# A graph and expert network on one core: two LSTM streams, and the ODE layer beside a VectorE recurrence

## The chip, the cores and the metric

The kernel runs on one core of a Trainium2 chip. A core has TensorE (matrix products, results in PSUM), VectorE (DVE), ScalarE (ACT), GpSimd (POOL) and SyncE (SP, which here starts the DMAs). Each engine runs its own list of instructions in order; they meet only at semaphores. The metric is the device time of one execution in microseconds (us). TensorE's clock is granted in two levels, 1.2 and 2.4 GHz; the profile gives the mean as a share of the higher.

## What is computed

Eight residual blocks over x of 16 batches x 512 nodes x 128 features. Each takes the layer norm of x and adds its result to x. Two of them matter here, the diffusion LSTM and the Euler steps of an ODE, and of a third the eigenvectors of the graph's Laplacian:

```python
# 1: diffusion LSTM
h = relu(einsum('ts,bsh->bth', adj, x @ Wg0 + bg0))
h = relu(einsum('ts,bsh->bth', adj, h @ Wg1 + bg1))
for p in range(1, 5):
    nw = T // p
    wins = h[:, :nw * p, :].reshape(B * nw, p, H)
    last = lstm_last(Wih[p-1], Whh[p-1], bih[p-1], bhh[p-1], wins)   # p steps
    h = h.at[:, arange(nw) * p + (p - 1), :].set(last.reshape(B, nw, H))
# 3: ODE, after the first expert layer
h = einsum('bnd,ed->bne', x, fc_in_w) + fc_in_b
for _ in range(8):
    f = alph * 0.5 * (adj @ h - h) + h @ w_eff - h + x0
    h = h + f / 8
# 5: spectral
_, U = eigh(L_norm)
```

## The kernel before

The whole network is one program. Nothing is loaded in between but weights: x stays in SBUF as X, 64 tiles of 128 nodes x 128 features (GT = 4 tiles a batch). The stages follow one another: the Laplacian is made tridiagonal; `diffusion_lstm`; the first expert layer, beside which VectorE and ScalarE count eigenvalues; in `eigenvectors` a recurrence for the vectors and their joining; the product with the reflections; `ode`; two expert layers with the spectral layer between; attention; the last expert layer.

`diffusion_lstm` runs a hardware loop over 8 pairs of batches. TensorE makes adj x (L2262), times the first weights (L2267 and L2268), times the second (L2273), times adj (L2279), and then the recurrences of p = 1 to 4. The 512 nodes of a pair's two batches are columns. `steps` lists eleven turns: p = 1 for each batch, then p = 2, 3, 4 with one turn for each t, both batches side by side, 2 x (512 // p) columns. A turn has three or four gates. For each, TensorE adds the input part (Wih, L2287, which reads HL at a stride of p columns) and, for t > 0, the state part (Whh, L2302). ScalarE puts the gate through a sigmoid or tanh into `gt` (L2336); VectorE makes the cell CC (L2224 to L2233), ScalarE its tanh (L2341), VectorE the state or, in a chain's last turn, the columns of HL (L2241). The next turn's state part waits for that. There are two sets of four PSUM banks (PG, PAB), and the input part of turn t + 1 goes into the other set while the gates of turn t are read. At the end TensorE turns HL around (L2310) and VectorE adds it to X. All of the pair's buffers exist once, and the next pair starts when `x_done` comes. An fp32 matmul is two passes, and the profile counts passes.

In `eigenvectors`, VectorE runs a recurrence over 512 nodes, for four eigenvalues a partition, from both ends of the matrix: q = d - lambda - e2 / q'. The forward and backward halves are 4 numbers each. Before it, DN is filled with the diagonals and e2 for all nodes (L908 to L916). A hardware loop over 32 blocks of 16 nodes copies a block of DN to `dn` (L923), does for each node STT, TT and RECIPROCAL for either half (L933, L937, L942) in `qr`, and copies `qr` to QR (L945). Behind it are operations on four rows of 512 (from L958), the scaling of V by G (L1016 to L1032) and the joining of the parts (from L1058). TensorE has nothing here.

`ode` rewrites the eight Euler steps as polynomials in M = L1 (the mixing matrix) with coefficients Gm and Fr (from powers R). Preparation: layer norm statistics of X (L1353); TensorE transposes L1 (L2458) and makes the products L2T, L3T, L6T (L2464), copied from PSUM by ScalarE (L2389), and small rows (L2495 to L2503). Then come 17 turns, g = -1 for the constant part and 0 to 15 for the batches: TensorE multiplies YT by Gm (L2551), transposes the next batch (L2557), applies M to UU (L2563), makes the next batch's L3T rows (L2570), applies M to VV, and makes the L6T rows. VectorE copies UU (L2517) and VV (L2526), normalises batch g + 2 (`normalize`, L1399), adds KC to X (L2523) and adds the result (L2530). ScalarE copies YT (L2539).

## Time and profile before

| | us |
|---|---|
| runs | 7629.35, 7630.39, 7633.64 |
| median | 7630.39 |
| the profiled execution: its own time | 7630.28 |
| its span in the trace | 7628.1 |
| TensorE busy | 5332.3 (70%) |
| VectorE busy | 4702.8 (62%) |
| ScalarE busy | 2291.0 (30%) |

No engine is busy throughout. The shares of the whole span say little, since the stages have different limits; they have to be read stage by stage. A row of stretches gives for each engine what it was busy for in one, and the granted clock. A row of the timeline gives the start of a run of like instructions, its length, the engine, the line, the operation, its operands and its shape; in square brackets, how long the engine had stood and what released it. "PEq", "DVEq" and "ACTq" there are the engines' own sequencers, which held the instruction back for a semaphore.

### The profile page before, as it was taken

Reading aid. Unit: us, or ns where it says so; the run is one execution under the profiler, and the core shown is the slowest. Engines: PE = TensorE matmul, PEld = TensorE weight load, DVE = VectorE, ACT = ScalarE, POOL = GpSimd, SP = SyncE. Lnnn points to the kernel's source line nnn. Section 1 sums busy time; section 2 is a strip of 40 time slices with the busy share of each in tenths; the row PEclk is TensorE's granted clock in tenths of the full one; section 3 lists DMA queues with packets and bytes.
Section 4 is the critical chain, followed back from the end, with each engine's and each line's share of the span. In section 5 each row is a group of like instructions: output and inputs, shape, how many; then the busy total and the mean of one; then the engine's idle time right before and its main releaser. Section 6 shows DMA issues by size and latency. Waiting matters only on the chain. (4 is left out here: it accounts for less than half of the span.)

```text
span 7628.1 us, 113557 instructions
## 1 busy us (share of the span) xinstructions
PE 5332.3 (70%) x33091; PEld 3818.8 (50%) x33091; DVE 4702.8 (62%) x29590; ACT 2291.0 (30%) x7310; POOL 17.9 (0%) x36
## 2 busy tenths in 40 slices
PE   5777666555555688869899940048966679966899
PEld 5656555555444344446566630025644247744676
DVE  7878888787887422249999999952135333342433
ACT  1222222222222233329699850001012023310333
POOL 0000000000000000000000000000000000000000
PEclk9999999999999988869999975579978879987799
DMA  0000000000000000010000000000001000000000
GB/s 35 2 2 2 2 2 2 1 1 1 1 1 1 18 0 0 0 48 5 4 5 5 5 1 0 0 7 1 1 6 40 1 11 0 0 8 12 0 0 22
DMA packets 23193, 47.92 MB, mean 6 GB/s; under 512 B 5673, under 2 KB 16322, under 8 KB 20930
## 3 DMA queue, kind: packets, MB, share of 16 engines
q1 hardware_dynamic: 22722, 42.40, 1.6%
q8 instruction: 202, 3.31, 0.2%
q14 instruction: 269, 2.20, 0.1%
HBM read 34.00 MB, written 8.39 MB: 6 GB/s over the span
## 5 line engine op out<-in xcount | busy, mean ns | idle before, releaser
L476 PE MATMUL h_M<-h_part,ones 128*128 128x2 f32 x1024 | 300.3, 363 | 575.9 <-DVE h_jd L384 575.9
L1746 DVE SCALAR_TENSOR_TENSOR f_ACC<-f_yp,f_CG,f_ACC 128x128 f32<-128x128 f32 x1024 | 288.2, 344 | 461.8 <-DVEq L1744 461.8
L476 PEld LDWEIGHTS h_M<-h_part,ones 128*128 128x128 f32 x1024 | 256.3, 311 | 619.6 <-DVE h_jd L384 619.6
L1691 PEld LDWEIGHTS f_yp<-f_W,f_hs 128*128 128x128 f32 x4096 | 490.0, 192 | 92.5 <-issue 91.8
L1625 PE MATMUL f_hp<-f_rows,f_W 128*128 128x512 f32 x1024 | 531.5, 601 | 5.1 <-ACT U L1635 3.1
L819 ACT ACTIVATE e_XD<-e_X,e_scal 128x60 f32<-128x60 f32 x2048 | 527.6, 333 | 17.5 <-DVEq L683 15.7
L1722 ACT ACTIVATE f_hs<-f_hp,f_b 128x512 f32<-128x512 f32 x512 | 347.6, 685 | 539.9 <-ACTq L1721 538.5
L471 PEld LDWEIGHTS h_ax<-h_XM,h_parts 128*128 128x128 bf16 x11520 | 508.8, 116 | 0.0
L1681 PE MATMUL f_hp<-f_XT,f_W 128*128 x1024 | 484.1, 600 | 33.0 <-PEq L1975 33.0
L1691 PE MATMUL f_yp<-f_W,f_hs 128*128 128x128 f32 x4096 | 493.5, 275 | 0.0
L436 ACT ACTIVATE h_VW<-h_v,h_s 128x8 f32<-128x8 f32 (+3 forms) x512 | 154.8, 302 | 1043.9 <-DVE h_s L388 1043.9
L456 PE MATMUL h_tot<-h_part,ones 128*128 128x2 f32 x1024 | 300.3, 363 | 227.7 <-DVE h_jb L311 227.7
L471 PE MATMUL h_ax<-h_XM,h_parts 128*128 128x3 bf16 x11520 | 425.5, 167 | 0.0
L456 PEld LDWEIGHTS h_tot<-h_part,ones 128*128 128x128 f32 x1024 | 256.3, 311 | 298.8 <-DVE h_jb L311 298.8
L1615 PEld LDWEIGHTS f_yp<-f_W,UT 128*128 128x128 f32 x2048 | 266.6, 194 | 188.8 <-issue 92.2
L1221 PE MATMUL q_PT<-ident,e_Z 128*128 128x128 f32 x16 | 3.6, 423 | 499.5 <-PEq L1052 499.5
L460 PE MATMUL h_sr<-h_sums,ones 128*128 128x1 f32 (+15 forms) x1024 | 314.8, 397 | 48.4 <-DVE h_sums L329 34.3
L1615 PEld LDWEIGHTS f_yp<-f_W,U 128*128 128x128 f32 x2048 | 268.6, 192 | 114.2 <-issue 93.2
L1615 PE MATMUL f_yp<-f_W,UT 128*128 128x128 f32 x2048 | 281.0, 281 | 41.4 <-ACT UT L1635 32.2
L432 ACT ACTIVATE h_s<-h_tot 128x1 f32<-128x1 f32 x512 | 87.6, 171 | 697.1 <-PE h_tot L456 697.1
L460 PEld LDWEIGHTS h_sr<-h_sums,ones 128*128 128x128 f32 x1024 | 257.3, 312 | 71.5 <-issue 44.8
L477 PE MATMUL h_tot<-h_tiny,ones 128*128 128x2 f32 x1024 | 289.8, 353 | 0.0
(681 smaller groups left out, 11729.6 us busy)
## 6 DMA issues: line engine op xcount, KB each, us to landing
f_S<-in_f_W SPq DMA_DIRECT2D x64, 128.0 KB, 2.3
X<-in_x SPq DMA_DIRECT2D x1, 4096.0 KB, 16.5
f_W<-in_f_W SPq DMA_DIRECT2D x2, 2048.0 KB
spill<-f_xts SPq DMA_DIRECT2D x16, 256.0 KB, 2.0
f_rows<-spill SPq DMA_DIRECT2D x16, 256.0 KB, 2.6
f_W<-in_f_W SPq DMA_DIRECT2D x4, 1024.0 KB
out<-X SPq DMA_DIRECT2D x1, 4096.0 KB, 11.1
h_A<-in_adj SPq DMA_DIRECT2D x1, 1024.0 KB, 5.7
```

The source lines that it names most:

```text
L456: nc.tensor.matmul(tot[q][:, 0:2], C.ones[:, :], part[:, 0:2], start=False, stop=True).then_inc(tot_out, 1)
L460: nc.tensor.matmul(sr[:, 0:1 + 4 * j], C.ones[:, :], sums[:, 0:1 + 4 * j], start=True, stop=True).then_inc(sr_out, 1)
L471: ins = nc.tensor.matmul(ax[:, m, 0:3], A_part[:, b, m * P:(m + 1) * P], XB[:, q, b, 2 * XC + 1:2 * R2 + 2:2], start=(b == ph and n == 0), ...
L476: nc.tensor.matmul(dots, C.ones[:, :], part[:, 2:4], start=True, stop=True).then_inc(dots_out, 1)
L477: nc.tensor.matmul(tot[1 - q][:, 0:2], C.ones[:, :], tiny[:, :], start=True, stop=False)
L819: ins = nc.scalar.activation(XD[b][:, k, h, :], X[:, :], ACT.Identity, bias=scal[b][:, k, 2 * h:2 * h + 1])
L1615: ins = nc.tensor.matmul(self.yp[d % 3][:, 0:D], self.hs[unit % 2][:, j, i * P:(i + 1) * P], self.W2[:, unit % E * FC + j, :], start=(j == ...
L1625: nc.tensor.matmul(self.hp[s % 3][:, :], self.W1[:, e, j * P:(j + 1) * P], self.rows[:, g % 2, :], start=True, stop=True).then_inc(self.h_ ...
L1681: nc.tensor.matmul(hp[:, u % 2, c, :], W1[:, col // F, col % F:col % F + P], rows_t, start=True, stop=True).then_inc(h_full, 1)
L1691: ins = nc.tensor.matmul(yp[:, u % 2, k, :], hs[:, u % 2, c, k * P:(k + 1) * P], W2[:, u * UC + c, :], start=(c == 0), stop=(c == UC - 1))
L1722: nc.scalar.activation(hs[:, u % 2, c, :], hp[:, u % 2, c, :], func, bias=b1[:, u * UC + c:u * UC + c + 1]).then_inc(hs_full, 1)
L1746: ins = V_.scalar_tensor_tensor(ACC[:, k, :], yp[:, u % 2, k, :], CG[:, k * E + e:k * E + e + 1], ACC[:, k, :], ALU.mult, ALU.add)
```

## The change

**LSTM.** The loop over pairs is written out. The pairs are two streams, st = 0 and 1, with buffers of their own (XG, G, H1, Y1, HL, HH, CC, `tc`, `ig`, `gt`) and one set of four banks each, PG[st]. The table `order` gives all engines the same sequence: a stage of one stream, then the same stage of the other. The input part of a turn now stands in the same stage as its state part, behind a wait for the gates of the turn before (`gates_in`). Semaphores count up and are waited for at constants.

**Recurrence.** Each node is three dependent operations of 8 numbers, both halves at once, which write QR directly. DN and the block copies are gone. Two operations of 128x16x4 for each block of 16 (`diagonals`) give d - lambda; they stand in the middle of the block before. The loop is written out. The scaling of V by G stands ahead of the recurrence. The first operations behind it take D and LAM instead of DN.

**ODE.** `ode` becomes a class `Ode`, whose lists for TensorE, ScalarE and SyncE run in the block of the recurrence. `start` issues on VectorE, ahead of the recurrence, the statistics and the preparation of L1. The rest of VectorE's share is a generator, `vector`; `tick`, called behind every node of the recurrence and most operations behind it, issues a piece when due. A turn is TURN = 29 ticks. UU, VV, KC and the result (HS, two buffers) are copied by ScalarE; VectorE only normalises and adds twice. YT has one buffer instead of two. L1, L2T, L3, UU, VV, KC, HS, R, Fr lie in buffers of the eigenvectors (Z, U, UT, g1, g2). In the preparation the first two Fr rows stand ahead of the product L6T, the third behind it, and the sums Gm behind that.

In the diff, dve, pe, act are the engines.

```diff
+        stages = ["ax", "h1", "y", "h2"] + steps + ["out"]
+        order = [(2 * i + st, st, stage) for i in range(B // 4) for stage in stages for st in range(2)]
+        gate_order = lambda t: (0, 2, 3) if t == 0 else (1, 0, 2, 3)
...
-                        if t == 0:
-                            input_part(p, t, n, bb)
-                        else:
-                            for gi in (1, 0, 2, 3):
-                                nc.tensor.matmul(banks[t % 2][:, gi, 0:n], Whh[:, p - 1, gi * D:(gi + 1) * D], HH[:, 0:n],
-                                                 start=False, stop=True).then_inc(gates_made, 1)
-                        if t + 1 < p:
-                            input_part(p, t + 1, n, bb)
...
+                        if stage == steps[0]:
+                            pe.wait_ge(hl_in, 2 * pair + 2)
+                        elif t == 0:
+                            pe.wait_ge(hid_in, before[st] + 1)
+                        if t:
+                            pe.wait_ge(gates_in, read_at[pair, (p, t - 1, n, bb)])
+                        x = windows(st, p, t, bb)
+                        for gi in gate_order(t):
+                            out = bank[:, gi, 0:n]
                             o2 = out if bb is not None else out.rearrange("p (b n) -> p b n", b=2)
                             ins = nc.tensor.matmul(o2, Wih[:, p - 1, gi * D:(gi + 1) * D], x, start=True, stop=(t == 0))
                             if t == 0:
-                                ins.then_inc(gates_made, 1)
...
+                                ins.then_inc(gates_out, 1)
+                        if t:
+                            pe.wait_ge(hid_in, before[st] + 1)
+                            for gi in gate_order(t):
+                                nc.tensor.matmul(bank[:, gi, 0:n], Whh[:, p - 1, gi * D:(gi + 1) * D], HH[st][:, 0:n],
+                                                 start=False, stop=True).then_inc(gates_out, 1)
...
+                    side.start(dve)
+                    side.begin(dve)
...
+                    def diagonals(chunk):
+
+                        at = chunk * CH
+                        back = D[:, N - 1 - at:N - 1 - at - CH:-1] if at + CH < N else D[:, N - 1 - at::-1]
+                        made = []
+                        for h, d in zip(halves, (D[:, at:at + CH], back)):
+                            V_.tensor_tensor(dn[chunk % 2][:, :, h], held(d), shift, ALU.subtract).then_inc(ch, 1)
+                            made.append(done.next())
+                        return made
...
+                    for n in range(N):
+                        chunk, k = n // CH, n % CH
+                        before = R[:, n - 1, :] if n > 0 else one[:, :]
+                        if n > 0:
+                            dve.wait_ge(ch, r_made)
+                        V_.scalar_tensor_tensor(two(t8[:, :]), two(before), 1e20, EE[:, :, n:n + 1].broadcast_to([P, 2, NB]),
+                                                ALU.min, ALU.mult).then_inc(ch, 1)
+                        t_made = done.next()
+                        if k == 0:
+                            dn_now = max(dn_made)
+                        if k == CH // 2 and chunk + 1 < N // CH:
+                            dn_made = diagonals(chunk + 1)
+                        dve.wait_ge(ch, max(t_made, dn_now))
+                        V_.tensor_tensor(Q[:, n, :], t8[:, :], dn[chunk % 2][:, k, :], ALU.add).then_inc(ch, 1)
+                        dve.wait_ge(ch, done.next())
+                        V_.reciprocal(R[:, n, :], Q[:, n, :]).then_inc(ch, 1)
+                        r_made = done.next()
+                        side.tick()
...
-                            t_made, q_made = [], []
-                            for h in (slice(0, NB), slice(NB, 2 * NB)):
-                                if k > 0:
-                                    dve.wait_ge(ch, r_made[len(t_made)])
-                                V_.scalar_tensor_tensor(t8[:, h], qr[:, k, 1, h], 1e20, dn[:, k, 1, h], ALU.min, ALU.mult).then_inc(ch, 1)
-                                t_made.append(done.next())
-                            for n, h in enumerate((slice(0, NB), slice(NB, 2 * NB))):
-                                dve.wait_ge(ch, t_made[n])
-                                V_.tensor_tensor(qr[:, k + 1, 0, h], t8[:, h], dn[:, k, 0, h], ALU.add).then_inc(ch, 1)
-                                q_made.append(done.next())
-                            r_made = []
-                            for n, h in enumerate((slice(0, NB), slice(NB, 2 * NB))):
-                                dve.wait_ge(ch, q_made[n])
-                                V_.reciprocal(qr[:, k + 1, 1, h], qr[:, k + 1, 0, h]).then_inc(ch, 1)
-                                r_made.append(done.next())
-                        dve.wait_ge(ch, done.n)
-                        V_.tensor_copy(QR[:, ds(chunk * CH, CH), :, :], qr[:, 1:CH + 1, :, :]).then_inc(ch, 1)
...
+        for turn in range(-1, B + 1):
+            used = 0
+            if turn + 2 < B and turn + 2 >= 1:
+                if turn >= 0:
+                    dve.wait_ge(self.ty_out, 3 * (turn + 1))
+                for n in range(NB):
+                    ins = self.row_block(turn + 2, n)
+                    if n == NB - 1:
+                        ins.then_inc(self.x_full, 1)
+                    yield 1
+                    used += 1
+            if 0 <= turn < B:
+                xs = flat(self.X[:, turn * GT:(turn + 1) * GT, :])
+                dve.wait_ge(self.hs_in, 1)
+                V_.tensor_tensor(xs, xs, self.KC, ALU.add).then_inc(ch, 1)
...
+                yield 6
+                used += 6
+            if turn >= 1:
+                xs = flat(self.X[:, (turn - 1) * GT:turn * GT, :])
...
+                dve.wait_ge(self.hs_in, turn + 1)
+                V_.tensor_tensor(xs, xs, self.HS[(turn - 1) % 2], ALU.add).then_inc(self.added, 1)
+            yield self.TURN - used
...
+    def tick(self):
+
+        if self.pause > 0:
+            self.pause -= 1
+        if self.pause == 0:
+            self.pause = next(self.work, -1)
+
...
+            act.wait_ge(self.q_out, g + 2)
+            nc.scalar.copy(wide(self.UU), Q[:, :, 2 * D:3 * D]).then_inc(self.u_in, 1)
+            row(0)
+            act.wait_ge(self.v_out, g + 2)
+            nc.scalar.copy(wide(self.VV), Q[:, :, D:2 * D]).then_inc(self.v_in, 1)
+            row(1)
+            act.wait_ge(self.h_out, g + 2)
+            if g >= 2:
+                act.wait_ge(self.added, g - 1)
+            nc.scalar.copy(wide(self.HS[g % 2] if g >= 0 else self.KC), Q[:, :, 0:D]).then_inc(self.hs_in, 1)
+            row(2)
...
+        for half in range(2):
+            if half:
+                pe.wait_ge(self.fr_in, half)
+            nc.tensor.matmul(PR[0:1, :], self.fbC[:, :], R[:, 1 + 4 * half:5 + 4 * half, :].rearrange("p m d -> p (m d)"),
+                             start=True, stop=True).then_inc(self.frow_out, 1)
+        pe.wait_ge(self.l3_in, NB)
+        product(L3, L3T, self.l6t_out)
+        pe.wait_ge(self.fr_in, 2)
+        nc.tensor.matmul(PR[0:1, 0:D], self.fbC[:, :], R[:, 0, :], start=True, stop=True).then_inc(self.frow_out, 1)
```

VectorE in the recurrence, before: the start of a block. `e_dn` is the block of DN, `e_qr` holds q and 1/q.

```order
L923 COPY e_dn<-e_DN 128x256
L925 COPY e_qr<-e_qr 128x8
L933 SCALAR_TENSOR_TENSOR e_t<-e_qr,e_dn 128x4 [waits e_chain]
L933 SCALAR_TENSOR_TENSOR e_t<-e_qr,e_dn 128x4
L937 TENSOR_TENSOR e_qr<-e_t,e_dn 128x4 [waits e_chain] x2
L942 RECIPROCAL e_qr<-e_qr 128x4 [waits e_chain] x2
L933 SCALAR_TENSOR_TENSOR e_t<-e_qr,e_dn 128x4 [waits e_chain] x2
L937 TENSOR_TENSOR e_qr<-e_t,e_dn 128x4 [waits e_chain] x2
```

The same engine after, around the middle of a block in the ODE's turns (`X<-X,UT` adds the ODE's result held by HS, which lies in UT):

```order
L980 SCALAR_TENSOR_TENSOR e_t<-e_QR,e_EE 128x8 [waits e_chain]
L969 TENSOR_TENSOR e_dn<-e_D,e_LAM 128x16x4 x2
L988 TENSOR_TENSOR e_QR<-e_t,e_dn 128x8 [waits e_chain]
L990 RECIPROCAL e_QR<-e_QR 128x8 [waits e_chain]
L2562 TENSOR_TENSOR X<-X,UT 128x512 [waits g1_hs_in,g1_ch]
L980 SCALAR_TENSOR_TENSOR e_t<-e_QR,e_EE 128x8 [waits e_chain]
L988 TENSOR_TENSOR e_QR<-e_t,e_dn 128x8 [waits e_chain]
L990 RECIPROCAL e_QR<-e_QR 128x8 [waits e_chain]
L980 SCALAR_TENSOR_TENSOR e_t<-e_QR,e_EE 128x8 [waits e_chain]
L988 TENSOR_TENSOR e_QR<-e_t,e_dn 128x8 [waits e_chain]
L990 RECIPROCAL e_QR<-e_QR 128x8 [waits e_chain]
```

Six operations of 4 numbers a node became three of 8, each waiting for the one before it; the diagonals stand between the first and the second, and an ODE operation behind a node.

TensorE in the LSTM, before: p = 2 and the start of p = 3.

```order
L2287 MATMUL g_PAB<-g_HL,g_Wih 128x512 x4
L2302 MATMUL g_PAB<-g_HH,g_Whh 128x512 [waits g0_hid_full]
L2302 MATMUL g_PAB<-g_HH,g_Whh 128x512 x3
L2287 MATMUL g_PG<-g_HL,g_Wih 128x340 [waits g0_hid_full]
L2287 MATMUL g_PG<-g_HL,g_Wih 128x340 x2
L2287 MATMUL g_PAB<-g_HL,g_Wih 128x340 x4
L2302 MATMUL g_PAB<-g_HH,g_Whh 128x340 [waits g0_hid_full]
L2302 MATMUL g_PAB<-g_HH,g_Whh 128x340 x3
```

After: p = 2, t = 1, of either stream, which begins behind the three gates of t = 0 of each.

```order
L2340 MATMUL g_PG<-g_HL,g_Wih 128x512 [waits g0_gates_in]
L2340 MATMUL g_PG<-g_HL,g_Wih 128x512 x3
L2346 MATMUL g_PG<-g_HH,g_Whh 128x512 [waits g0_hid_in]
L2346 MATMUL g_PG<-g_HH,g_Whh 128x512 x3
L2340 MATMUL g_PG<-g_HL,g_Wih 128x512 [waits g0_gates_in]
L2340 MATMUL g_PG<-g_HL,g_Wih 128x512 x3
L2346 MATMUL g_PG<-g_HH,g_Whh 128x512 [waits g0_hid_in]
L2346 MATMUL g_PG<-g_HH,g_Whh 128x512 x3
```

The input part of t = 1 no longer stands ahead of the wait for the state in another set of banks; it waits for the gates to be read, and the same eight matmuls of the other stream follow before this stream's next turn.

VectorE in an ODE turn, before:

```order
L2517 COPY g_UU<-g_Q 128x512 [waits g1_q_out]
L1399 TENSOR_SCALAR g_XG<-X,g_mean,g_rstd 128x128 x4
L2523 TENSOR_TENSOR X<-X,g_KC 128x512 [waits g1_h_free]
L2526 COPY g_VV<-g_Q 128x512 [waits g1_v_out]
L2530 TENSOR_TENSOR X<-X,g_Q 128x512 [waits g1_ch,g1_h_out]
```

ScalarE in an ODE turn, after (UT holds UU and VV, U holds KC):

```order
L2599 COPY g_YT<-g_TY 128x512 [waits g1_ty_out]
L2605 COPY UT<-g_Q 128x512 [waits g1_v_out]
L2599 COPY g_YT<-g_TY 128x512 [waits g1_ty_out]
L2610 COPY U<-g_Q 128x512 [waits g1_h_out]
L2599 COPY g_YT<-g_TY 128x512 [waits g1_ty_out]
L2602 COPY UT<-g_Q 128x512 [waits g1_q_out]
```

The copies for which TensorE waits have moved to ScalarE's list, and what stays with VectorE stands between nodes of the recurrence.

## Rows read from the trace of the kernel before

**Rows 1.** Stretches: start:end, us; busy PE, PEld, DVE, ACT, POOL; clock; DMA, GB/s.
```profile
2550.00:3314.00 764.00, 621.93 (x1520) 313.02 (x1520) 183.93 (x361) 243.49 (x448) 0.17 (x1) 0.86 0.00 0
...
4519.40:5016.00 496.60, 0.00 (x0) 0.00 (x0) 457.99 (x3518) 2.12 (x3) 0.00 (x0) 0.50 0.00 0
...
5133.60:5234.00 100.40, 68.29 (x178) 31.40 (x179) 38.29 (x155) 13.16 (x23) 0.00 (x0) 0.81 0.04 13
5234.00:5632.60 398.60, 378.84 (x1802) 252.74 (x1800) 60.12 (x127) 28.11 (x48) 0.00 (x0) 0.99 0.00 1
```

**Rows 2.** Timeline of TensorE in the LSTM: start, us, operation, count [idle before <-releaser].
```profile
2609.03 3.79 PE L2287 MATMUL g_PG<-g_HL,g_Wih 128*128 128x340 f32 x8
2612.64 2.46 PE L2302 MATMUL g_PG<-g_HH,g_Whh 128*128 128x340 f32 x8
...
2626.04 3.79 PE L2287 MATMUL g_PG<-g_HL,g_Wih 128*128 128x256 f32 x8
2629.64 1.91 PE L2302 MATMUL g_PG<-g_HH,g_Whh 128*128 128x256 f32 x8
...
2639.53 1.94 PE L2310 MATMUL g_PAB<-ident,g_HL 128*128 128x128 f32 x8 [2.63 <-PEq L2307]
...
2754.16 2.07 PE L2273 MATMUL g_PAB<-g_W,g_H 128*128 128x128 f32 x16
2756.31 7.10 PE L2279 MATMUL g_PAB<-g_AT,g_Y 128*128 128x512 f32 x16
```

**Rows 3.** Timeline of a p = 1 step: ScalarE, VectorE, then TensorE.
```profile
2582.07 0.69 ACT L2336 ACTIVATE g_gt<-g_PG,g_bih 128x512 f32<-128x512 f32 x1 [0.41 <-ACTq L2334]
...
2583.42 0.69 DVE L2241 TENSOR_TENSOR g_HL<-g_gt,g_tc 128x512 f32<-128x512 f32 x1 [0.92 <-DVEq L2235]
...
2584.26 4.55 PE L2287 MATMUL g_PG<-g_HL,g_Wih 128*128 128x512 f32 x6 [2.32 <-PEq L2297]
```

**Rows 4.** Timeline of VectorE: start of a block of the recurrence, and the next block.
```profile
4531.43 0.29 DVE L923 COPY e_dn<-e_DN 128x256 f32 x1 [0.34 <-DVE e_qr L918]
4531.64 0.16 DVE L925 COPY e_qr<-e_qr 128x8 f32<-128x8 f32 x1
4531.84 0.23 DVE L933 SCALAR_TENSOR_TENSOR e_t<-e_qr,e_dn 128x4 f32<-128x4 f32 x2
...
4532.44 0.23 DVE L933 SCALAR_TENSOR_TENSOR e_t<-e_qr,e_dn 128x4 f32<-128x4 f32 x2
...
4542.65 0.29 DVE L923 COPY e_dn<-e_DN 128x256 f32 x1 [0.66 <-DVE e_QR L945]
```

**Rows 5.** Timeline of VectorE while eigenvalues are counted beside an expert layer.
```profile
3660.01 0.34 DVE L1646 SCALAR_TENSOR_TENSOR X<-f_yp,f_CB,X 128x128 f32<-128x128 f32 x1
3660.27 0.21 DVE L697 TENSOR_TENSOR e_u<-e_XD,e_PB 128x60 f32<-128x60 f32 x1
...
3660.72 0.27 DVE L708 SCALAR_TENSOR_TENSOR e_PB<-e_PB,e_scal,e_u 128x60 f32<-128x60 f32 x1
```

**Rows 6.** Timeline of VectorE behind the recurrence.
```profile
4888.94 3.64 DVE L958 TENSOR_TENSOR e_g<-e_QR,e_DN 128x2048 f32<-128x2048 f32 x1 [0.59 <-PEq L897]
...
4944.14 0.43 DVE L1016 TENSOR_SCALAR e_t<-t_G 128x512 f32<-128x512 f32 x1
...
4954.93 0.21 DVE L1058 TENSOR_SCALAR s_tol<-e_sc 128x1 f32<-128x1 f32 x1 [0.43 <-PEq L949]
```

**Rows 7.** Timeline of the ODE layer's preparation: VectorE's statistics, then TensorE.
```profile
5149.05 3.86 DVE L1353 BATCH_NORM_STATS2 g_ln_st<-X  x16 [0.31 <-issue]
...
5162.82 3.68 PE L2458 MATMUL g_Q<-ident,g_L 128*128 128x128 f32 x16 [3.58 <-DVE g_L L2409]
...
5227.00 12.80 PE L2551 MATMUL g_Q<-g_Fr,g_yrow 1*128 1x384 f32 x24 [1.15 <-PEq L2381]
```

**Rows 8.** ODE turns: timeline of TensorE, and one line of the code by its instructions.
```profile
5256.96 8.01 PE L2551 MATMUL g_Q<-g_Gm,g_YT 128*128 128x384 f32 x24 [0.68 <-ACT g_YT L2539]
...
L2530 DVE TENSOR_TENSOR X<-X,g_Q x16: 686/687/689, 5276.6 to 5630.5; 128x512 f32<-128x512 f32 x16
```

More of the change, by code:

```diff
@@ L1034, in _ @@
+                    dve.wait_ge(ch, done.n)
                     dve.sem_clear(ch)
                     done.restart()
[L1037 to L1058 removed]
@@ L1183, in _ @@
[L1183 to L1187 removed]
+                        V_.tensor_tensor(Z[:, jb, :], Z[:, jb, :], t1[:, :], ALU.subtract).then_inc(ch, 1)
+                        side.tick()
+                        dve.wait_ge(ch, done.next())
```

1166 lines of the change are left out of this document (604 added, 562 removed).

## The prediction, made before the changed kernel had run

> **What bounds the kernel now.** I read the table by stretches first [rows 1]. It shows three stretches in which one engine works and the rest stand. From 2550 to 3314 us, the diffusion LSTM, TensorE is busy 622 of 764 us at a mean level of 0.86 (one of its levels, 2.4 or 1.2 GHz, is granted at a time), and neither VectorE (184) nor ScalarE (243) is near its limit. From 4519.4 to 5016 VectorE is busy 458 of 497 us, and TensorE does nothing. From 5234 to 5632.6, the ODE turns, it is the reverse: TensorE 379 of 399 us at 0.99, VectorE 60. From 5133.6 to 5234 both take turns. The change touches these four; the other stages keep their code.
>
> The timeline inside the LSTM shows why TensorE stands there. A p = 1 recurrence step is matmuls, three gate activations, cell product, tanh, hidden product (0.69), and only then the next step's matmuls, 2.32 us after TensorE ran dry [rows 3]. The last chain ends with 2.63 us of idle time ahead of the transposes of a pair's result [rows 2].
>
> In the recurrence of the eigenvectors a step is three dependent pairs of 128x4 operations; it takes 0.61 us (4531.84 to 4532.44), and the time is that between dependent operations, about 0.2 each, not that of the numbers [rows 4]. A block of 16 steps takes 11.22 us (4531.43 to 4542.65), 16 x 0.606 = 9.7 of it in steps and 1.5 in copies and the loop's end.
>
> **The change, LSTM.** TensorE's work for a pair, at the high level, from rows [rows 2]: a pass of 512 contiguous columns is 7.10 / 16 = 0.44 us. adj x (16 passes) 7.1, h1 (8) about 3.9, y 2.1, h2 7.1, p = 1 (12 passes) 5.3. In the later chains the strided Wih reads cost 3.79 for 8 passes, with 340 as with 256 columns, and I take as much for p = 2; Whh costs 2.46 (340), 1.91 (256) and, as a pass of 512, 3.6. So p = 2: 14 Wih passes 6.6 and Whh 3.6, 10.2; p = 3: 22 passes 10.4 and 2 x 2.46, 15.3; p = 4: 30 passes 14.2 and 3 x 1.91, 19.9; transposes 1.9. Sum 72.8. Neighbouring rows overlap (2609.03 to 2612.64 is 3.61 for a row of 3.79), 0.15 for each of some 20 blocks, so 70. Now a pair takes 764 / 8 = 95.5 with 622 / 8 = 77.7 of it busy, the excess over 70 being the lower level [rows 1]. The change removes no pass. It gives TensorE the other stream's stage while one waits.
>
> Does that cover each wait? A stage of p = 2 to 4 is 5.4 to 7 us of matmuls in the other stream; the chain behind a stage (last gate, cell, tanh, state) leaves TensorE dry for 2.3 to 2.6 us now [rows 2, 3]. Covered. At p = 1 a stage is six passes, 2.6 us, and ScalarE needs three gates and a tanh, 4 x 0.69 = 2.8, and waits some 0.2 for the cell: 3.0 [rows 3]. ScalarE is late by 0.4 in each of four stages, and the outputs expose about as much: some 2 us for each two pairs, 8 for all. The new waits are that a Wih part of step t now waits for the gates of t-1 to be read (it has no second bank any more) and stands in front of Whh; behind it is queued only the other stream, whose 5 us have passed. Filling and draining the two streams costs 3 each. 8 x 70 + 8 + 6 = 575 instead of 761 from 2550 to the end: **-186**. The bounds: if the low level stays as it is now, 8 x 77.7 + 8 + 6 = 636, -125; with no exposed wait at all 560, -201. I take 575, because in every stretch where TensorE is fed it is at the high level (0.99 to 1.00 in the ODE turns [rows 1]).
>
> Of the strided reads: the rows show 0.47 us a pass at 340 and 256 columns where contiguous ones take 0.31 and 0.24 [rows 2]. The Trainium skill, "SBUF — State Buffer", under "Door 1: The DMA port swizzle", says that fp32 can be strided by up to 4 for free. This case's rows disagree. By the page the p = 3 and 4 passes would cost 10.7 less a pair and the LSTM would be some 85 us shorter still; the rows decide.
>
> **The change, recurrences and ODE.** The ODE's TensorE work goes beside VectorE's recurrence. Start, on VectorE: the G and V scaling comes forward (4944.14 to 4954.93: 10.4 net [rows 6]); `bn_stats` is four groups of 16, about 3.9 each, 15.6 with what lies between [rows 7]; ODE preparation 3. With 0.9 for waits on either side of the statistics (like places wait 0.43 and 0.59 [rows 6]) TensorE starts its transposes at 4519.4 + 0.5 + 10.4 + 0.9 + 15 + 0.9 + 3.2 = 4550; the layer norm's eight small operations, the root and the first diagonals bring the recurrence to start at 4555. Removed: the building of DN, 11 us up to 4531.03, and 32 times 1.5 us between blocks, of which 0.4 comes back as the two diagonals' operations: about 50 in all [rows 4].
>
> TensorE's setup takes 64.2 (5162.82 to 5227.00 [rows 7]). Beside the recurrence it is slower, since VectorE answers only every so many steps: TensorE comes to the F rows some 37 us after its start, at 4587, but VectorE reads the first at its 67th step, at 4555 + 67 x 0.61 + 2 = 4598: 10 lost. Then VectorE comes to the third F row at its 71st step and stands 12 us, because TensorE makes it behind the 14 us of L6T. Only then follow 36 sums for Gm at 0.2 us, 7 us, longer than TensorE's small rows last, and turn -1 waits for what VectorE does behind them: 7 lost. 64 + 17 = 81. Turn -1 takes 30.0 (5227.00 to 5256.96 [rows 7, 8]), and a turn 353.9 / 15 = 23.6 (first and last of 16 adds [rows 8]).
>
> VectorE's own turn is 29 steps. A step with three operations of 8 numbers: the one measured 128x8 operation takes 0.16 and the next dependent one follows after 0.20 [rows 4]. So 0.61 again, 17.7 for 29. ODE's rows and two adds are 60.1 / 16.9 - 2 x 0.69 = 2.2 a turn [rows 1], of which a part fills the 0.05 us gaps, as an inserted 0.34 us operation moves the next by 0.26 [rows 5]. 19.7: less than 23.6. **TensorE sets the pace**; VectorE waits 4 us a turn for `ty_out`, and the 50 us that its recurrence has saved are hidden behind that pace.
>
> All times here are those of the trace of before, as if the LSTM were not shorter. Turn 0 of TensorE begins at 4550 + 81 + 30 = 4661. VectorE's turn 13 begins when TensorE's turn 12 has ended, at 4661 + 13 x 23.6 = 4968, and the last of the 512 steps is 29 steps later, 19.7 us: the recurrence ends at 4987. (VectorE alone would need 512 x 0.61 + 13 + 15 x 2 = 355, and end at 4910.) TensorE's last turn has no products ahead (-7) and ends at 4661 + 16 x 23.6 - 7 = 5031, under the part behind the recurrence. That part runs from 4888.94 to 5016, less the 10.8 that came forward, 116 [rows 1, 6], and carries some 3 of the ODE's last turns: 4987 + 119 = 5106. So the stage ends **90 later**, and the stage 5133.6 to 5632.6, 499 us, is gone: **-409**.
>
> UU, VV and the result move from VectorE to ScalarE, which is otherwise idle there; its operation on 512 columns takes 0.69, as VectorE's does [rows 3], so no term.
>
> **Sum.** 7628.1 - 186 - 409 = 7033; with the 2.2 between the span and that run's 7630.28, which is the median of the runs within 0.1: **7035 us**.
>
> **Rivals.** (a) VectorE sets the pace. Nearest row against me: a dependent operation of 128x60 takes 0.21 to 0.27 [rows 5], and if an 8-number step is 3 x 0.27 to 0.31, 0.93, the 512 steps take 476 + 45 and the recurrence ends at 5075, 88 later: 7123. It decides from (23.6 - 2) / 29 = 0.74 us a step. Against it is the 128x8 row. 12%. (b) TensorE stays on alternating levels in the LSTM because the streams keep leaving it small holes: 636 instead of 575, 7096. The holes that went with the low level before were 2.3 to 2.6 us long [rows 2, 3], and few of those remain. 9%. The Trainium skill, "TensorE: Matmul & The Clock Gate", under "A second HAM failure mode: psum-queue depth-cycling", tells of such oscillation from micro-idles between groups; this trace's 0.86 agrees with oscillation, and no row shows how short a hole may be. (c) The ODE turns run at the low level, since VectorE's pace leaves holes in them: of 23.6 us a turn 22.4 are matmuls [rows 1], at half the clock 46, and 13 turns before the recurrence's end add 13 x 22.4 = 291: 7326. Against it: that hole-bearing turn is at the high level now. 3%. (d) Slower than before: TensorE and VectorE in lockstep. If each turn needed VectorE's 19.7 and then TensorE's 46 at the low level, with setup and turn -1 at that level too (+80, turn 0 at 4741), TensorE would end at 4741 + 16 x 66 = 5797, 691 behind my 5106: 7726. The point from which it decides is a turn of 60 us (4741 + 16 x 60 = 5701, 595 later). The waits contradict it (rows are made one whole turn ahead). 2%. (e) Better: stages that were exposed are covered fully and setup waits of 29 don't appear: 7035 - 15 - 30 = 6990. 12%. (f) The change does not do what it says, the streams run one after the other because a wait for reading gates orders them: 761 instead of 575, 7221. 2%. My forecast has 60%.
>
> **Numbers.** About 0.2% (15 us) is what a measurement can tell. The range 6985 to 7125 takes in (e), (b) and (a), and leaves out (c), (d), (f) and tails. Only (d) ends above: faster 0.97, same 0.01, slower 0.02.
>
> **What would show it.** In the profile after: LSTM of 575 us with a granted level of 1.0 (wrong: 0.9 or less); recurrence steps of 0.61 us (wrong: 0.74 or more); ODE turns of 23.6 us on TensorE with VectorE waiting 4 us for it; less the LSTM's 186, turn 0 near 4475, the recurrence's end near 4801 and the next expert stage's start near 5038. The prediction is wrong above all if 8-number operations cost more, or if TensorE's setup stretches beyond 81 us, since each microsecond there counts in full.

## The result, and the profile after

The changed kernel takes 7035.36 us (median of four runs, 7029.39 to 7042.54) against 7631.52 us in the runs beside it. The ratio is 0.9219, with a 95% interval of 0.9203 to 0.9235. The forecast was 7035 us with a range of 6985 to 7125. The profiled execution has a span of 7032.6 us.

The first view is again the table of stretches: start and end, length, busy time (instructions) of PE, PEld, DVE, ACT and POOL, granted clock, DMA share and GB/s. The four rows of the changed kernel are the LSTM, the whole stage of the eigenvectors with the ODE in it, 13 ODE turns in its midst, and the product with the reflections.

```profile
2550.00:3120.00 570.00, 561.88 (x1520) 281.97 (x1520) 181.03 (x363) 237.73 (x448) 0.00 (x0) 0.98 0.00 0
4326.80:4912.50 585.70, 450.69 (x1978) 285.05 (x1978) 452.41 (x2182) 72.40 (x126) 0.00 (x0) 0.88 0.01 3
4466.10:4773.40 307.30, 295.42 (x1405) 196.10 (x1404) 226.30 (x1254) 44.38 (x78) 0.00 (x0) 1.00 0.00 1
4912.50:5035.00 122.50, 78.69 (x296) 51.65 (x296) 36.32 (x39) 0.00 (x0) 0.54 (x2) 0.83 0.00 0
```

Beside [rows 1]: the LSTM's 1520 matmul passes are the same, but 761 us have become 570. The idle time of 142 us is 8, and the busy time for the same passes is 562 us instead of 622, at a mean granted level of 0.98 instead of 0.86. The stretch of 497 us in which TensorE did nothing is one in which it works 451 of 586 us, and the 499 us of ODE behind it are gone.

The boundaries of the stages (mostly the first instruction of the next one) compare so:

| | before | after | difference |
|---|---|---|---|
| first statistics behind the LSTM | 3316.6 | 3124.8 | -191.8 |
| start of the eigenvectors' last stage | 4519.4 | 4326.8 | -192.6 |
| end of the recurrence | 4887.9 | 4793.5 | -94.4 |
| first expert layer behind the ODE (statistics) | 5633.9 | 5037.4 | -596.5 |
| span | 7628.1 | 7032.6 | -595.5 |

**The LSTM.** The timeline of TensorE over one change of pairs, to set beside [rows 2] and [rows 3] (start, us, engine, line, operation, count, idle time before):

```profile
2690.86 1.09 PE L2326 MATMUL g_PG<-ident,g_HL 128*128 128x128 f32 x8 [1.34 <-DVE g_HL L2287]
2691.78 13.90 PE L2301 MATMUL g_PG<-g_AT,g_XG 128*128 128x512 f32 x32
...
2713.84 3.84 PE L2314 MATMUL g_PG<-g_W,g_H 128*128 128x128 f32 x32
2717.52 13.90 PE L2320 MATMUL g_PG<-g_AT,g_Y 128*128 128x512 f32 x32
2731.25 19.46 PE L2340 MATMUL g_PG<-g_HL,g_Wih 128*128 128x512 f32 x44
2750.55 3.59 PE L2346 MATMUL g_PG<-g_HH,g_Whh 128*128 128x512 f32 x8
2753.99 3.76 PE L2340 MATMUL g_PG<-g_HL,g_Wih 128*128 128x512 f32 x8
```

The row of 44 passes is all of p = 1 for both streams and the start of p = 2, without a pause. What is left of waiting for others (TensorE's waits in the stretch of the LSTM: who waited <- for whom, us in total, times, longest):

```profile
PE g_PG L2326 <- DVE g_HL L2287: 5.4, 4, 1.3
PE g_PG L2301 <- DVE g_XG L1427: 3.7, 1, 3.7
PE g_PG L2340 <- DVE g_HL L2287: 0.6, 4, 0.2
```

**Recurrence and ODE.** A node of the recurrence on VectorE, and an ODE piece between two nodes:

```profile
4360.38 0.30 DVE L2484 TENSOR_SCALAR g_XG<-X,g_mean,g_rstd 128x128 f32<-128x128 f32 x1
4360.59 0.16 DVE L980 SCALAR_TENSOR_TENSOR e_t<-e_QR,e_EE 128x8 f32<-128x8 f32 x1
4360.79 0.17 DVE L988 TENSOR_TENSOR e_QR<-e_t,e_dn 128x8 f32<-128x8 f32 x1
4360.99 0.20 DVE L990 RECIPROCAL e_QR<-e_QR 128x8 f32<-128x8 f32 x1
4361.23 0.17 DVE L980 SCALAR_TENSOR_TENSOR e_t<-e_QR,e_EE 128x8 f32<-128x8 f32 x1
```

A step is 0.64 us (4360.59 to 4361.23), where [rows 4] had 0.61. TensorE meanwhile (preparation, turn -1, turn 0):

```profile
4354.55 3.52 PE L2622 MATMUL g_Q<-ident,e_Z 128*128 128x128 f32 x16 [2.75 <-DVE e_Z L2450]
...
4405.32 1.87 PE L2657 MATMUL g_PR<-e_g,g_fbC 128*1 128x512 f32 x2 [11.99 <-DVE e_g L2519]
...
4434.17 15.72 PE L2678 MATMUL g_Q<-e_g,U 1*128 1x384 f32 x24 [4.97 <-DVEq L2539]
...
4466.83 8.01 PE L2678 MATMUL g_Q<-g_Gm,g_YT 128*128 128x384 f32 x24 [0.68 <-ACT g_YT L2599]
...
4490.47 8.01 PE L2678 MATMUL g_Q<-g_Gm,g_YT 128*128 128x384 f32 x24 [0.68 <-ACT g_YT L2599]
```

and VectorE's two long waits in the stage:

```profile
DVE g_XG L2484 <- PE g_TY L2697: 58.2, 14, 12.7
DVE e_g L2524 <- PE g_PR L2662: 13.1, 1, 13.1
```

The turn keeps the 23.6 us of [rows 8] (4466.83 to 4490.47), and VectorE waits 14 times for TensorE's products ahead: 12.7 us before its turn 0, and (58.2 - 12.7) / 13 = 3.5 in each turn after it.

### The profile page after: what moved, and what is told of

Its sections match the earlier page's. It is cut to its first block and busy times, and to the rows that moved or that the text cites. A ratio compares the mean times of both kernels' runs of the same rounds, so it can differ in the third digit from the quotient of the medians.

```text
span 7032.6 us, 110639 instructions
## 1 busy us (share of the span) xinstructions
PE 5280.7 (75%) x33091; PEld 3792.1 (54%) x33091; DVE 4595.9 (65%) x27972; ACT 2313.6 (33%) x7361; POOL 17.9 (0%) x36
## 5 line engine op out<-in xcount | busy, mean ns | idle before, releaser
L2340 PE MATMUL g_PG<-g_HL,g_Wih 128*128 128x256 f32 (+2 forms) x624 | 288.5, 619 | 0.6 <-DVE g_HL L2287 0.6
```

The costliest lines, as they stand in the source:

```text
L2340: ins = nc.tensor.matmul(o2, Wih[:, p - 1, gi * D:(gi + 1) * D], x, start=True, stop=(t == 0))
```

## The experiments

All are edits of the changed kernel; they are compared with its 7035 us, and where the difference is small, by the traces' stages.

**1. The LSTM of before.** `diffusion_lstm` is replaced by the function of before.

```diff
-        order = [(2 * i + st, st, stage) for i in range(B // 4) for stage in stages for st in range(2)]
+                with pe.Fori(0, B // 2) as i:
...
```

> The changed kernel with the LSTM function of before (one stream, loop over pairs); all else as changed. If the two parts of the change are independent, it takes what the LSTM gained, 192 us by the traces, more than the changed kernel: 7035 + 192 = 7227 us. If the ODE and recurrence part owed something to the new LSTM (code, buffers), the sum would differ from that by more than 15 us.

Measured: 7233.64 us (7230.91 to 7236.37). The 198 us are the trace's 192 within the spread, and the recurrence takes the same 435 us (4547.7 to 4982.6; 4358.7 to 4793.3 in the changed kernel). So the two parts are independent.

**2. The ODE ahead of the recurrence.** No pieces between nodes.

```diff
                     side.begin(dve)
+                    side.finish()
+                    dve.wait_ge(side.added, B)
...
-                        side.tick()
```

> The changed kernel with the whole ODE list run ahead of the recurrence instead of beside it (no pieces between the nodes). Theory that the gain is the overlap: TensorE 66 + 30 + 371 us alone, then 512 steps of 0.64 and 10 us of diagonals, then 116: 7035 + 363 = 7398 us, and a step shows 0.64 us without anything beside it. Rival, that the new recurrence itself gave the gain: below 7150 us.

Measured: 7400.72 us, one run; its last two expert layers, which no edit touches (end of this section), took the same 1367 us as the changed kernel's. The overlap is worth 365 us. The new recurrence by itself ran from 4826.7 to 5158.8, 332 us (0.65 a node with the diagonals) where the old one took 357. So 25 us, the 11 of DN and some 4 of the statistics (below) are saved without overlap; all the rest is overlap. TensorE's turn here, with no node beside it, takes the same 23.64 us (4618.48 to 4642.12) as beside the recurrence.

**3. Pairs of four again.** Six operations a node instead of three.

```diff
-                        V_.reciprocal(R[:, n, :], Q[:, n, :]).then_inc(ch, 1)
-                        r_made = done.next()
+                        for m, h in enumerate(halves):
+                            dve.wait_ge(ch, q_pair[m])
+                            V_.reciprocal(R[:, n, h], Q[:, n, h]).then_inc(ch, 1)
+                            r_pair.append(done.next())
```

> The changed kernel with each node's three operations of 8 numbers split again into six of 4 (two chains, as before). Theory that TensorE sets the pace of the recurrence: same time, 7035 within 10 us, and VectorE's wait for TensorE a turn goes from 4.2 to 5 us, because pairs take 0.61 a step and single operations of 8 took 0.64. Rival, that the operation of eight numbers is what made the recurrence fast: slower by 512 steps times its saving, at least 50 us.

Measured: 7032.05 us (7031.55 to 7032.63). The same time. The wait grew, but only from 58.2 to 62.0 us in all: a node takes 0.61 us, but a row of 128x128 between nodes now costs 0.18 us net (a node with it takes 0.79) where it cost 0.10 (4359.86 to 4360.59, 0.73) between single operations. The operation of eight numbers gives this kernel nothing; the recurrence's own chain does not set its time.

**4. Streams in turn.** Same buffers, same written-out code, no alternation.

```diff
-        order = [(2 * i + st, st, stage) for i in range(B // 4) for stage in stages for st in range(2)]
+        order = [(2 * i + st, st, stage) for i in range(B // 4) for st in range(2) for stage in stages]
```

> The changed kernel with the same two sets of buffers and the same written-out code, but each pair's stages in one piece instead of alternating with the other stream's. Theory that the alternation covers the waits and keeps the high clock level: the waits come back, and the input part no longer runs ahead, some 100 us a pair, LSTM 800 us, total 7270. Rival, that writing out the loop and waiting on constants brought the gain: below 7080 us.

Measured: 7217.87 us, one run, 183 more (again with 1367 us in the last expert layers). The stretch of the LSTM and the timeline of TensorE in it show the waits and the lower level that came back:

```profile
2550.00:3303.00 753.00, 622.09 (x1520) 301.10 (x1520) 184.51 (x368) 244.33 (x450) 0.00 (x0) 0.89 0.00 0
...
2669.20 2.84 PE L2340 MATMUL g_PG<-g_HL,g_Wih 128*128 128x512 f32 x6 [0.69 <-ACT g_HL L2365]
2674.08 2.84 PE L2340 MATMUL g_PG<-g_HL,g_Wih 128*128 128x512 f32 x6 [2.04 <-DVE g_HL L2287]
2678.95 2.96 PE L2340 MATMUL g_PG<-g_HL,g_Wih 128*128 128x512 f32 x6 [2.04 <-DVE g_HL L2287]
2682.70 3.86 PE L2340 MATMUL g_PG<-g_HL,g_Wih 128*128 128x512 f32 x8 [0.78 <-ACT g_gt L2371]
...
2692.82 3.28 PE L2340 MATMUL g_PG<-g_HL,g_Wih 128*128 128x340 f32 x6 [2.83 <-DVE g_HL L2287]
```

From one pair's adj x to the next one's it is 91.4 to 94.8 us, on average 93.6 (2552.12 to 3207.16 for seven), where it was 95.5 before the change. I had expected 100, because the input part no longer runs ahead, and had not counted that the next pair's first stages need nothing of this one's last. TensorE is busy for 622 us at a level of 0.89, which is the busy time of before: the two buffers and the written-out code give nothing there, and the 60 us of the higher level come with the alternation as the covered waits do. Of the LSTM's 192 us, 183 are the alternation's and 9 the rest's.

**5. Turns of 24 nodes.**

```diff
-    TURN = 29
+    TURN = 24
```

> The changed kernel with 24 nodes a turn of the ODE in place of 29. Theory that TensorE sets the pace at 23.64 us a turn and VectorE waits for it: VectorE's own share of a turn shrinks by 5 x 0.64 us and its wait grows by as much, but all 17 turns now fall inside the recurrence, so its end is tied to TensorE's last turn: 27 nodes behind 4839 us, at 4857 instead of 4793; 7035 + 61 = 7096 us. Rival, that VectorE's own work sets the pace: within 10 us of 7035.

Measured: 7097.02 us (7091.58 to 7100.12), as expected to 1 us. VectorE's waits for TensorE's products ahead grew from 58.2 to 103.9 us, and it waited 15.9 us for results that ScalarE had to copy. The recurrence took 498 us instead of 435 and ended at 4861.4 (it had begun 4.6 us later than the changed kernel's).

**6. Turns of 36 nodes, and the root moved.** The first turns have 36 nodes, those from the eleventh on 24, and the last pieces of the ODE stand between the levels of the joining. With 36 nodes a turn, more ODE turns lie behind the recurrence. ScalarE's root, which VectorE needs there, stood in ScalarE's list behind the ODE's last turn, and had to go between two turns.

```diff
-            yield self.TURN - used
+            yield (36 if turn < 11 else 24) - used
...
             row(2)
+            if g == 12:
+                length()
...
                     while size < N:
+                        side.piece()
```

> The changed kernel with 36 nodes a turn for the first turns and 24 from the eleventh on (behind the recurrence an operation is longer than a node), ScalarE's root for the vectors' length put between its ODE turns 12 and 13 instead of behind the last, and the last pieces of the ODE put between the levels of the joining. Theory that VectorE's waits of 58 us in all are what the recurrence's end waits for: the waits nearly go, a turn is 24 us, the recurrence ends at 4731 instead of 4793; 7035 - 62 + 3 = 6975 us. Rival, that TensorE then starves for rows or for ScalarE behind the root: 7010 or more.

Measured: 6993.56 us (6987.69 to 6995.7), between the theories. The recurrence took 379 instead of 435 us and VectorE's waits fell from 58.2 to one of 8.2. I had taken VectorE's own turn as 19.5 us, with all 14 waits alike; without the long first one it is 20.1, and so 36 nodes are 24.6 us: VectorE set the pace, and the recurrence was 7 us longer than expected. And TensorE stood behind the root:

```profile
4799.16 5.36 PE L2700 MATMUL g_Q<-UT,g_L1T 128*128 128x128 f32 x32 [12.27 <-ACT UT L2610]
```

ScalarE could not copy UU before it had done the root at 4798.4, so the ODE's end came late, and VectorE stood 3.5 us for it in the joining. From the end of the recurrence to the last scaling it was 127.3 us instead of 119.0. So of the 19 us by which the span fell short (59 less expected, 40 measured), 7 lie in the recurrence and 5 behind it (8 where I had allowed 3). The other 7 lie outside: the stage began 4.4 us later, and 3 us are in the stages behind it.

**7. The preparation in another order.** VectorE reads the F rows as soon as they are there, TensorE makes the third ahead of the product L6T, and the sums for Gm run beside that product.

```diff
-            yield 17
+            yield 17 if k < 2 else 6
...
-        pe.wait_ge(self.l3_in, NB)
-        product(L3, L3T, self.l6t_out)
         pe.wait_ge(self.fr_in, 2)
         nc.tensor.matmul(PR[0:1, 0:D], self.fbC[:, :], R[:, 0, :], start=True, stop=True).then_inc(self.frow_out, 1)
...
+        pe.wait_ge(self.l3_in, NB)
+        product(L3, L3T, self.l6t_out)
+        row_sum(1, L3T)
```

> The changed kernel with the ODE's preparation in another order, TURN = 29 as it was: the F rows are read by VectorE as soon as they are there (the node at which they come is 53 instead of 64), the third of them is made ahead of the product L6T, and the Gm sums run beside that product. Theory that TensorE's preparation counts in full for the end: 12 us less from its start to turn -1 (67 instead of 79.6), and all that follows 12 earlier: 7023 us. Rival, that the preparation is off the path because VectorE has 13 us of waiting less, too: if VectorE set the pace it would be 7035 - 13 - 5, or nothing at all if the end hangs on something else.

Measured: 7013.38 us (7008.85 to 7017.75), 22 less. From TensorE's first transpose to turn -1 it is now 65.3 us instead of 79.6, and turn -1 takes 30.0 instead of 32.7:

```profile
4358.23 3.49 PE L2630 MATMUL g_Q<-ident,e_Z 128*128 128x128 f32 x16 [2.75 <-DVE e_Z L2450]
...
4398.69 1.02 PE L2665 MATMUL g_PR<-e_g,g_fbC 128*1 128x512 f32 x2 [1.69 <-DVE e_g L2508]
...
4423.49 13.04 PE L2689 MATMUL g_Q<-e_g,U 1*128 1x384 f32 x24 [1.29 <-DVEq L2547]
```

That is 17.0 us, and the recurrence (4362.4 to 4779.9) is 17.1 shorter: each microsecond of the preparation counts in full. The time alone does not decide against the rival, whose sum is 7017 us. The trace does: VectorE's wait of 13.1 us for the third F row is gone, but it still waits 14 times for TensorE's products ahead, 55.6 us in all, 10.0 before turn 0 and again 3.5 in each of 13 turns. The profiled executions differ by 16.8 us (spans of 7032.6 and 7015.8); the other 5 us of the medians' difference are within the spread of the runs.

**8. Packed windows.** VectorE copies the columns t, t + p, ... of HL side by side.

```diff
+                        if t == p - 1 and bb != 0 and q in PACKED:
+                            dve.wait_ge(hid_in, turn_at[pair, stage] + 1)
+                            for u in range(q):
+                                V_.tensor_copy(packed(st, q, u).rearrange("p (b n) -> p b n", b=2),
+                                               windows(st, q, u, None)).then_inc(win_in, 1)
...
+                        if p in PACKED:
+                            x = packed(st, p, t).rearrange("p (b n) -> p b n", b=2)
```

> The changed kernel with the input windows of p = 3 and p = 4 copied to contiguous columns by VectorE (7 copies a pair, into H1, which is free then), so that the Wih matmuls read contiguous columns. What is computed is the same. Theory from the rows of before that a pass of Wih costs 0.47 us because of its stride of 3 or 4 columns: the passes fall to 0.31 and 0.24, as Whh's, and the LSTM by 8 x 10.7 = 86 us: 6949. By the Trainium skill, SBUF - State Buffer, strides up to 4 are free and the 0.47 has another cause: then 7035 or a little more, for the copies.

Measured: 6942.16 us (6938.43 to 6942.95). The passes fell to what Whh's take:

```profile
2640.64 2.45 PE L2365 MATMUL g_PG<-g_H,g_Wih 128*128 128x340 f32 x8
2642.92 2.45 PE L2371 MATMUL g_PG<-g_HH,g_Whh 128*128 128x340 f32 x8
...
2648.28 3.26 PE L2365 MATMUL g_PG<-g_H,g_Wih 128*128 128x256 f32 x14 [1.62 <-DVE g_H L2300]
2651.38 1.89 PE L2371 MATMUL g_PG<-g_HH,g_Whh 128*128 128x256 f32 x8
```

8 passes of 256 columns take 1.89 instead of 3.79 us. The Trainium skill, "SBUF — State Buffer", "Door 1: The DMA port swizzle", has strides of up to 4 fp32 free; for TensorE's moving operand this run decides against it. TensorE's busy time in the LSTM fell by 562 - 482 = 80 us, and the LSTM by 68, since it waits 13 us for copies. The remaining 25 us of the result are in stages that the edit does not touch, 20 of them in the last expert layers (below). So the agreement with the expected 6949 is luck: the stage itself gave 68 us of the expected 86.

**9. The three together.**

```diff
-            yield 17
+            yield 17 if k < 2 else 6
...
-            yield self.TURN - used
+            yield (36 if turn < 11 else 24) - used
...
+        PACKED = (3, 4)
```

> The changed kernel with the three edits of the runs before together: packed windows for p = 3 and 4, the ODE's preparation in the new order, 36 nodes a turn with ScalarE's root between its turns 12 and 13. If their gains add: VectorE is rid of both its 58 us and its 13 us of waiting, the recurrence ends some 70 us earlier than in the changed kernel, and with 93 less in the LSTM it is 6871 us. If TensorE's last turns (35 us of them behind the root) end the stage instead, 6880 to 6890.

The edits of 6, 7 and 8 are in it whole. Measured: 6878.49 us (6871.68 to 6886.09), a ratio of 0.9008 (0.8993 to 0.9023) to the kernel before: the fastest of the study, and ahead of the changed kernel by 157 us, 20 of which lie in the last expert layers (below). The time is between the two that I had expected, 6871 and 6880 to 6890. The recurrence took 363 us, 72 less than in the changed kernel. Behind it the end of the stage still depends a little on TensorE:

```profile
4766.11 0.69 DVE L2599 TENSOR_TENSOR X<-X,UT 128x512 f32<-128x512 f32 x1 [4.87 <-ACT UT L2651]
...
4781.81 3.32 PE L1253 MATMUL q_PT<-ident,e_Z 128*128 128x128 f32 x16 [16.45 <-PEq L34]
```

TensorE's last ODE matmuls end at 4765.4, and VectorE stands 4.87 us in the midst of the joining for their result. Then it finishes the joining, and TensorE waits 16.45 us for it. So the joining closes the stage, up to 4.87 us later than it could.

**10. All three, with pairs of four.** The edit of 3 on kernel 9.

```diff
-                        V_.reciprocal(R[:, n, :], Q[:, n, :]).then_inc(ch, 1)
+                            V_.reciprocal(R[:, n, h], Q[:, n, h]).then_inc(ch, 1)
```

> The kernel before it in this list, with each node's three operations of 8 numbers split into six of 4. With TensorE setting the pace this split gave 3 us. Where VectorE sets the pace, a step of 0.61 instead of 0.64 us counts 512 times, 15 us, less some 6 us because pieces between the nodes hide less well: 9 us faster than the kernel of eight numbers. Rival, that TensorE's end is what counts also here: same within 4 us.

Measured: 6887.59 us (6876.97 to 6899.84): not told apart from kernel 9 by the time. By the traces the recurrence took 358 instead of 363 us, so half of what I expected is there, and it is smaller than the spread. That the median is 9 us higher does not come from the edit: the last expert layers took 1370 us in this trace and 1347 in kernel 9's.

**11. Packed windows for p = 2 too.** The edit of 8, with one chain more.

```diff
+        PACKED = (2, 3, 4)
```

> The changed kernel with packed windows for p = 2, 3 and 4. Against the run with p = 3 and 4 alone (6942 us) it tells what a stride of 2 costs a pass of 512 columns: rows of before show 0.47 against 0.45 us, so 14 passes a pair save at most 8 x 14 x 0.02 to 0.04 = 2 to 5 us, and two copies of 0.7 us a pair stand in VectorE's list: 6940 within 5 us, no difference that counts.

Measured: 6963.67 us (6960.79 to 6969.37), 21 more than kernel 8, against the expectation. The trace does not put it on the edit: the LSTM ended at 3052.7 instead of 3057.0, 4 us earlier as expected, and the recurrence ended 2 us earlier. TensorE's busy time in the LSTM fell by 6 us more. What is longer lies in the last expert layers: 1368 us (5579.0 to 6946.9) against 1347.

**12. A fourth operation a node.** The copy makes each node's chain one operation longer; the result stays the same.

```diff
+                        dve.wait_ge(ch, done.next())
+                        V_.tensor_copy(z8[:, :], t8[:, :]).then_inc(ch, 1)
...
-                        V_.tensor_tensor(Q[:, n, :], t8[:, :], dn[chunk % 2][:, k, :], ALU.add).then_inc(ch, 1)
+                        V_.tensor_tensor(Q[:, n, :], z8[:, :], dn[chunk % 2][:, k, :], ALU.add).then_inc(ch, 1)
```

> The changed kernel with a fourth dependent operation of 8 numbers a node: a copy between the first and the second. 512 x 0.2 = 102 us of VectorE's time are added. Theory that VectorE waits 4.16 us a turn for TensorE: a turn of VectorE grows from 19.5 by 5.8 to 25.3 us and from there sets the pace against TensorE's 23.64, the first turn begins 13 us later because TensorE's preparation waits for VectorE's reads, and the recurrence ends 13 + 13 x 1.7 + 5.8 = 40 us later: 7075 us. So 60 of the 102 us are hidden. Rival, that the recurrence's length sets the time as it did before the change: 7137 us.

Measured: 7082.26 us (7081.41 to 7087.58), 47 more. The recurrence ran from 4363.9 to 4850.4, 487 us instead of 435. VectorE's waits for TensorE's products ahead fell from 58.2 to 7.7: of 102 us added, 50 went into the waits and 52 came out at the end. Of the 12 us by which the recurrence grew more than I had expected (52 instead of 40), 9 are those of the wait again: 3.5 and not 4.16 in each of 13 turns.

**The stages that no edit touches.** From the first to the last of the 1024 operations by which the last two such expert layers add their results (line, engine, operation, count, durations in ns, first and last start), for the changed kernel, kernel 8 and kernel 10:

```profile
L1774 DVE SCALAR_TENSOR_TENSOR f_ACC<-f_yp,f_CG,f_ACC x1024: 339/342/352, 5650.6 to 7017.6; 128x128 f32<-128x128 f32 x171
```

```profile
L1774 DVE SCALAR_TENSOR_TENSOR f_ACC<-f_yp,f_CG,f_ACC x1024: 339/342/352, 5578.7 to 6925.8; 128x128 f32<-128x128 f32 x171
```

```profile
L1786 DVE SCALAR_TENSOR_TENSOR f_ACC<-f_yp,f_CG,f_ACC x1024: 340/343/352, 5513.3 to 6883.0; 128x128 f32<-128x128 f32 x171
```

That is 1367, 1347 and 1370 us for the same code. The stretches of the changed kernel and of kernel 8 over it:

```profile
5650.00:6340.00 690.00, 612.60 (x3138) 429.43 (x3137) 244.24 (x822) 197.34 (x304) 0.82 (x3) 0.92 0.01 2
6340.00:7017.00 677.00, 598.93 (x3208) 435.42 (x3206) 263.34 (x814) 212.82 (x327) 0.14 (x1) 0.90 0.01 3
```

```profile
5578.00:6268.00 690.00, 606.35 (x3178) 425.45 (x3177) 248.04 (x830) 197.34 (x304) 0.82 (x3) 0.94 0.01 2
6268.00:6926.00 658.00, 584.25 (x3167) 422.04 (x3166) 260.31 (x809) 212.84 (x327) 0.14 (x1) 0.91 0.01 4
```

The shorter one has the higher granted clock (0.94 and 0.91 against 0.92 and 0.90) and less busy time for as many passes. In the traces of all fourteen kernels these layers took 1363 to 1371 us but for kernels 8 and 9, where they took 1347. It is not the kernel alone that decides: the four runs of kernel 10 lie at 6877 and 6878 and at 6897 and 6900 us, with a mean granted level of 0.938 in the shorter two and 0.935 in the longer two. So differences of up to some 20 us between two of these kernels can come from there, and that is why the edits of 8, 9, 10 and 11 are judged by their own stages. What decides which of the two it is was not tried.

## Why the prediction was right, point by point

**The LSTM: -186 forecast, -192 measured.** The work of a pair, 70 us at the high level, was 562 / 8 = 70.2. The clock did stay up (0.98). What failed is the small term, idle time of 14 us where 8 were measured: the four exposed p = 1 stages at 0.4 us. I added the rows' lengths, 4 x 0.69, but neighbouring operations on ScalarE start 0.59 apart, as the row behind the gate of [rows 3] at 2582.07 shows in the trace of before:

```profile
2582.66 0.62 ACT L2341 ACTIVATE g_tc<-g_CC 128x512 f32<-128x512 f32 x1
```

That is 2.4 for four, less than TensorE's 2.6, and TensorE's row of 44 passes has no pause. I also misread one length that did no harm: a stage with t = 0 of p = 2 to 4 has six passes, 2.8 us, and not 5.4 to 7; it was covered all the same. Experiment 4 shows that the alternation is the cause, of the covered waits and of the higher level both, and experiment 8 that the strided reads were priced rightly by the rows.

**The recurrence: the pace is TensorE's.** The forecast said so, with a recurrence that ends at 4801 on the new time scale; it ended at 4793.5, and six of the eight microseconds are the LSTM's. Experiments 5 and 12 show it by the time, and experiment 7 by its waits; in experiment 6, where VectorE's turn was made longer than TensorE's, it no longer holds. VectorE's own turn was forecast at 19.7 us and is 23.64 - 3.5 = 20.1. Two errors in it nearly cancel: a step is 0.64 instead of 0.61 (the reciprocal of 8 numbers takes 0.20 us, and the operation behind it starts 0.24 after it), which is 0.9 us more for 29 steps, and all that stands between the nodes comes to 1.5 us instead of 2.0, although the forecast had left the diagonals out of the turn. So VectorE waits 3.5 a turn instead of 4. The saving of "about 50" in the recurrence itself adds up to 46 from the prediction's own terms, and 36 were measured (experiment 2); it was forecast to be hidden, so the sum does not depend on it. The rival by which 8-number operations cost 0.93 a step was far off; its point of decision was 0.74.

**The preparation: 81 forecast, 79.6 measured**, with its parts: 10 forecast for the F rows (11.99), 12 for VectorE in front of L6T (13.1), 7 for the last small rows (4.97). Turn -1 was forecast at 30.0 and took 32.7. Its first matmuls took 15.72 us at a granted level of 0.50 instead of the 12.80 of [rows 7] at 0.61. TensorE had stood for 5 us before them, and in experiment 7, where it stood for 1.3, they took 13.04 at 0.61. Against this, TensorE's first transposes came 3 us earlier than forecast (4354.55, against 4550 - 192.6 = 4357.4), because the statistics took 12.5 us and not 15. So turn 0 began at 4466.8 where the forecast, on the new time scale, has 4468.4: right within 2 us, with three misses of 1 to 3 us that cancel.

**The end of the stage: 90 later forecast, 89 measured** (the last scaling of the vectors ends at 4912.5, which is 5105.1 with the 192.6 of the stages ahead, against 5015.7). What I left out is behind it. The gap up to the copy of the first transposes grew from 4.2 to 7.0 us and the reflections' products took 2 more (111.3 to 113.3, copy to copy). So the ODE part gave -404, not -409. This miss of 5 and the LSTM's of 6 cancel: that the median lies within 1 us of the forecast is luck of that size, and the untouched stages move by more.

**The sum** was built on one profiled execution, and its stages held within 6 us each. The rivals are ruled out by the same rows: the step of 0.64 us against (a), 0.98 in the LSTM against the alternating level (b), the granted level of 1.00 in the 13 turns against the low-level turns (c), the turn of 23.64 against lockstep (d), the 79.6 us of preparation with its waits against (e), and the 570 us of the LSTM against (f).

## What to carry to other kernels

Where two engines take turns at being idle, give the idle one independent work in the same queue order, and then ask at once which of the two sets the pace of the merged loop: here the waits at one line (58 us on VectorE, 14 times) named it, and what shortened the pacing engine's chain counted in full, while three or six operations a node made no difference. Choose the number of host steps a merged turn gets so that both engines' turns are about equal; 24, 29 and 36 nodes gave 7097, 7035 and 6994 us, the last with ScalarE's root moved as well. Look at the time of a pass by operand layout: taking a stride of 3 or 4 out of the moving operand shortened its stage by 68 us, about as much as the two edits of the pace together (42 and 22 us). And compare two builds stage by stage: layers that no edit touched differed by 20 us.

## What the runs showed of the hardware

- A TensorE pass with a moving operand read at a stride of 3 (340 columns) or 4 (256 columns) takes 0.47 us; packed, it takes 0.31 and 0.24. At a stride of 2 (512 columns) it is 0.47 against 0.45 (3.76 and 3.59 us for 8 passes), and packing gave only 4 us in 112 passes. The three strided passes take the same time though they read 512, 340 and 256 columns; what they have in common is that each walks over the same 1024 columns.
- Three dependent VectorE operations of 8 numbers take 0.64 us, three dependent pairs of 4 numbers 0.61. An independent 0.30 us operation between two nodes costs 0.10 us net in the first and 0.18 in the second.
- The `bn_stats` of 64 tiles in one written-out row took 12.5 us, where in four groups of a loop they took 16.7 (5136.23 to 5152.9).
